# Second layers of a gated expert network on one core: two product sizes, one fp32 expert instead of three, and a reordered start of the first half

## The reference, cut to what matters

```python
B, L, DM, H, E, HD = (512, 64, 768, 4, 8, 384)
scores = einsum('bld,d->bl', x, aw); scores = where(x.sum(-1) != 0, scores, -inf)
feature = einsum('bl,bld->bd', softmax(scores), x)
g_h = relu(einsum('bd,hdk->bhk', feature, gW1) + gb1)
gate = softmax(einsum('bhk,hke->bhe', g_h, gW2) + gb2)[arange(b), D]
h1 = relu((einsum('bd,edk->ebk', feature, eW1) + eb1[:, None]) * inv1[:, None] + bn1_b[:, None])
h2 = relu((einsum('ebk,eko->ebo', h1, eW2) + eb2[:, None]) * inv2[:, None] + bn2_b[:, None])
rep = einsum('be,ebo->bo', gate, h2)
out = softmax((einsum('bo,hoc->bhc', rep, hW) + hb)[arange(b), D])
```

## Time and profile before

| what | value |
|---|---|
| median of 3 runs | 584.44 us (584.1 to 585.29) |
| the profiled execution's own time | 583.16 us |
| its span | 581.4 us |
| mean granted TensorE clock | 0.954 |
| PE busy | 515.3 us, 89% |
| DVE busy | 479.8 us, 83% |
| ACT busy | 460.1 us, 79% |
| POOL busy | 88.6 us, 15% |
| read from HBM | 167.32 MB |

### The profile page before, as it was taken

The page is one execution under the profiler, slowest core; times in us unless marked ns, Lnnn a source line. Parts: engine busy times, 40 slices in busy tenths (PEclk is TensorE's granted clock), DMA queues, the critical chain, the costliest instruction groups (busy, mean ns, idle before and its releaser), DMA issues.

```text
span 581.4 us, 10779 instructions
## 1 busy us (share of the span) xinstructions
PE 515.3 (89%) x3974; PEld 407.1 (70%) x3974; DVE 479.8 (83%) x917; ACT 460.1 (79%) x959; POOL 88.6 (15%) x130
## 2 busy tenths in 40 slices
PE   0476556879999999999999999999999999999995
PEld 0111112335987888878888888889889998999894
DVE  6899998998998897979999999664477686768673
ACT  5899999897999788988999899655566666666662
POOL 3100000002113020211121211112212222222200
PEclk9967888589999999999999999999999999999999
DMA  8999999998999999999999974545546756575620
GB/s 313 377 400 403 402 399 402 401 394 331 407 389 398 385 391 393 390 393 391 362 340 369 377 268 123 173 144 164 166 139 187 208 167 195 166 211 165 193 82 0
DMA packets 52053, 168.02 MB, mean 289 GB/s; under 512 B 4629, under 2 KB 4757, under 8 KB 52001
## 3 DMA queue, kind: packets, MB, share of 16 engines
q1 hardware_dynamic: 35344, 100.68, 45.2%
q0 software_dynamic: 16512, 66.27, 34.7%
q10 hardware_dynamic: 144, 0.39, 0.2%
HBM read 167.32 MB, written 0.00 MB: 288 GB/s over the span
## 4 chain that ended last, share of the span: by engine, by line
PE 49%; DMA 30%; DVE 14%; issue 5%; ACT 2%; SPq 0%; POOL 0%; DVEq 0%; ACTq 0%
DMA xring<-in_r_x_dram 29%; PE banks L957 9%; PE banks L947 8%; PE banks L949 8%; PE banks L948 8%; DVE prod_out L680 6%; PE banks L956 5%; DVE wlo L668 4%; PE banks L1034 4%; PE banks L1003 3%; PE banks L954 2%; PE banks L955 1%; DMA wraw<-in_L_rec_gW_dram 1%; DVE h L771 1%; ACT copy_out L457 1%
## 5 line engine op out<-in xcount | busy, mean ns | idle before, releaser
L680 DVE CUSTOM_DVE_ANT_0 prod_out<-xring,aw_bc 128x768 bf16<-128x768 f32 x256 | 233.3, 948 | 8.6 <-DMA xring<-in_r_x_dram 7.0
L457 ACT ACTIVATE copy_out<-xring 128x768 bf16<-128x768 f32 x256 | 212.8, 833 | 11.4 <-DMA xring<-in_r_x_dram 10.4
L668 DVE TENSOR_TENSOR wlo<-wraw,whi 128x1152 fp32r<-128x1152 f32 x106 | 142.6, 1351 | 32.9 <-ACT whi L442 32.8
L442 ACT ACTIVATE whi<-wraw 128x1152 fp32r<-128x1152 f32 x106 | 122.8, 1159 | 49.6 <-PE banks L949 27.2
L947 PE MATMUL banks<-feat,whi 128*128 128x256 f32 x432 | 124.6, 288 | 1.9 <-ACT h L499 0.6
L949 PE MATMUL banks<-feat,wlo 128*128 128x256 f32 x432 | 122.2, 283 | 0.0
L948 PE MATMUL banks<-feat,whi 128*128 128x256 f32 x432 | 122.1, 283 | 0.0
L1034 PE MATMUL banks<-xring,pwin 128*32 128x384 f32 (+1 forms) x1024 | 112.6, 579 | 9.6 <-ACT pwin L475 9.6
L422 POOL DMA_DIRECT2D wraw<-in_L_rec_eW_dram x90 | 68.5, 761 | 246.0 <-DVE wlo L668 240.1
L957 PE MATMUL banks<-feat,whi 128*128 128x512 f32 x240 | 86.4, 396 | 0.0
L947 PEld LDWEIGHTS banks<-feat,whi 128*128 128x128 f32 x432 | 82.8, 192 | 2.9 <-ACT w2raw L501 1.0
(11 more groups left out here) (118 smaller groups left out, 565.6 us busy)
## 6 DMA issues: line engine op xcount, KB each, us to landing
xring<-in_r_x_dram SPq DMA_DIRECT2D x128, 768.0 KB, 8.5
wraw<-in_L_rec_eW_dram POOLq DMA_DIRECT2D x90, 576.0 KB, 5.1
wraw<-in_L_rec_gW_dram POOLq DMA_DIRECT2D x16, 576.0 KB, 4.8
w2raw<-in_L_rec_eW_dram POOLq DMA_DIRECT2D x6, 576.0 KB, 8.4
aw_bc<-in_L_rec_aw_dram ACTq DMA_DIRECT2D x1, 384.0 KB, 5.4
w2raw<-in_L_rec_gW_dram POOLq DMA_DIRECT2D x1, 48.0 KB, 5.5
h<-in_L_rec_eb_dram POOLq DMA_DIRECT2D x1, 24.0 KB, 5.3
h<-in_L_rec_bn_g_dram POOLq DMA_DIRECT2D x1, 24.0 KB, 5.1
```

Source lines behind the costliest of these rows:

```text
L442: nc.scalar.activation(whi[:, split_slot(u), :, :], wraw[:, raw_slot(u), :, :], ACT.Copy).then_inc(hi_ready, 1)
L457: nc.scalar.activation(copy_out[:, t % 2, :], x_in[:, r % RING_ROUNDS, j, i, :], ACT.Copy, accum_out=rowsum[:, r % 2, t:t + 1]).then_inc(s ...
L668: nc.vector.tensor_tensor(wlo[:, split_slot(u), :, :], wraw[:, raw_slot(u), :, :], whi[:, split_slot(u), :, :].bitcast(F32), ALU.subtract) ...
L680: nc.vector.tensor_tensor_reduce(out=prod_out[:, t % 2, :], in0=x_in[:, r % RING_ROUNDS, j, i, :], in1=aw_bc[:, :], scale=1.0, scalar=0.0, ...
```

## The change

Four edits. `NATIVE` goes from 3 to 1, so experts 1 and 2 of chunk 0 get split second layers and the split experts' panel order. In chunk 1 the second-layer panels of experts 0 to 6 become wide; for that h1's high and low halves are put beside each other in one tensor (`h1s`), the tiles get a join on DVE, and the relu moves into the gating operation. Before the slot loop ACT and DVE get another order. The head's wait names another semaphore.

```diff
-NATIVE = 3
+NATIVE = 1
...
-            c, kind, _ = PANELS[panel]
-            return c == NCH - 1 and kind in "ab"
+            c, kind, q = PANELS[panel]
+            return c == NCH - 1 and kind in ("a" if q == E - 1 else "abc")
...
-        h1_hi = sb("h1_hi", [P, KT, CHUNK], F32R)
-        h1_lo = sb("h1_lo", [P, KT, CHUNK], F32R)
+        h1s = sb("h1s", [P, KT, 2, CHUNK], F32R)
+        h1_hi, h1_lo = h1s[:, :, 0, :], h1s[:, :, 1, :]
...
             softmax_exp(FIRST_ROUNDS - 1)
+            place_probs(FIRST_ROUNDS - 1)
             split_hi(0)
-            place_probs(FIRST_ROUNDS - 1)
             split_hi(1)
             copy_rows(1)
-            sum_rows(FIRST_ROUNDS, to_score(0)[:1])
             for g in range(2):
                 features_hi(1, g)
-            sum_rows(FIRST_ROUNDS, to_score(0)[1:])
+            sum_rows(FIRST_ROUNDS, to_score(0))
...
                 for m in range(MT):
-                    t = MT * "ab".index(kind) + m
+                    if kind == "c":
+                        part, col = h2[:, m, :], N1 + HT * q + m
+                    else:
+                        t = MT * "ab".index(kind) + m
+                        part, col = h1[:, t, :], KT * q + t
                     dve.wait_ge(part_ready, joined_count(panel, m))
-                    nc.vector.scalar_tensor_tensor(out=h1[:, t, :], in0=banks[:, bank_of(panel, m), 0:CHUNK],
-                                                   scalar=scale[:, KT * q + t:KT * q + t + 1], in1=h1[:, t, :],
+                    nc.vector.scalar_tensor_tensor(out=part, in0=banks[:, bank_of(panel, m), 0:CHUNK],
+                                                   scalar=scale[:, col:col + 1], in1=part,
                                                    op0=ALU.mult, op1=ALU.add).then_inc(joined, 1)
...
-                dve.wait_ge(z_read, read_count(panel_of(c, "c", q), MT - 1))
-                nc.vector.tensor_tensor(h2[:, :, :], h2[:, :, :],
-                                        gate_bc.unsqueeze(1).to_broadcast([P, HT, CHUNK]),
-                                        ALU.mult).then_inc(gated_ready, 1)
+                gates = gate_bc.unsqueeze(1).to_broadcast([P, HT, CHUNK])
+                panel = panel_of(c, "c", q)
+                if is_wide(panel):
+
+                    dve.wait_ge(joined, joined_count(panel, MT - 1))
+                    nc.vector.scalar_tensor_tensor(out=h2[:, :, :], in0=h2[:, :, :], scalar=0.0, in1=gates,
+                                                   op0=ALU.max, op1=ALU.mult).then_inc(gated_ready, 1)
+                else:
+                    dve.wait_ge(z_read, read_count(panel, MT - 1))
+                    nc.vector.tensor_tensor(h2[:, :, :], h2[:, :, :], gates, ALU.mult).then_inc(gated_ready, 1)
...
             split_lo(0)
-            split_lo(1)
             copy_rows(1)
-            score_tiles(FIRST_ROUNDS, to_score(0)[:1])
             for g in range(2):
                 features_lo(1, g)
-            score_tiles(FIRST_ROUNDS, to_score(0)[1:])
+            split_lo(1)
+            score_tiles(FIRST_ROUNDS, to_score(0))
...
-                        a_hi, a_lo = h1_hi, h1_lo
+                        a_hi, a_lo, a = h1_hi, h1_lo, h1s
                     else:
-                        a_hi, a_lo = feat_hi[:, c, :, :], feat_lo[:, c, :, :]
+                        a_hi, a_lo, a = feat_hi[:, c, :, :], feat_lo[:, c, :, :], feat[:, c, :, :, :]
...
-                            last = wide_products(bank, whi[:, slot, k, cols], wlo[:, slot, k, cols], feat[:, c, kk, :, :],
+                            last = wide_products(bank, whi[:, slot, k, cols], wlo[:, slot, k, cols], a[:, kk, :, :],
                                                  kk == 0, kk == KT - 1)
...
                 if c:
 
-                    pe.wait_ge(joined, joined_count(panel_of(c, "b", E - 1), MT - 1))
+                    pe.wait_ge(z_read, read_count(panel_of(c, "b", E - 1), MT - 1))
```

## The result

The changed kernel takes 587.5 us (median of 5 runs, 587.17 to 587.85) against 584.1 us (583.56 to 585.29): ratio 1.0058, 95% interval 1.0046 to 1.0069, so 3.4 us slower. The profiled execution took 587.46 us with a span of 585.6 us, 4.2 us longer than that of before.

What follows compares the result with a forecast made beforehand. The prediction took DVE's amount of work to set when slot 50 ends, with PE alone the bound later. Its terms, +5.5 - 1.2 + 0 = +4.3 us on 584.44, gave 588.7 us, range 583.6 to 593.

Steps and rivals of the forecast that it cites:

- What bounds the kernel: x's loads to 176 us, PE from 206 to 265, DVE's work from 265 to 362, PE alone from 450 to 560.
- the rival in which it can't: Before slot 50, DVE's idle time can't be used, so most of 16.3 us shows: +13.5, 598 us; chance 0.08.
- the one in which PE stays the bound: Between 206 and 362 us DVE's extra work is hidden and PE's savings count: -3.8 us, 580.6; chance 0.12.
- NATIVE and the layout: Before slot 50, 11.4 + 4.9 us more DVE work, less idle time and overlap, ends that slot 5.5 us later.
- the overlap: On DVE before slot 50, 20 added back-to-back instructions overlap by some 0.08 us each, taking off 1.6 us.
- The layout: DVE's copy to h1_hi slows from 548 to 958 ns; twelve copies before slot 50 add 4.9 us.
- The wide second layers: In chunk 1, wide second-layer panels save 1.0 to 1.5 us, taken as 1.2, with DVE's joins covered.
- The start: Reordering before the slot loop gives 0 (bounds -1.2 and +0.6), as a load of x ends the stretch at 175.6 us.
- Cost: nothing: In chunk 1, the wide second layers' joins and the relu inside the gating were claimed to cost nothing.
- Seven panels: Seven second-layer panels of chunk 1 were counted as becoming wide, saving 0.14 to 0.21 us each.
- The sum: Whole kernel: +5.5 before slot 50, -1.2 in chunk 1 and 0 for the start make +4.3 us.
- The level: Whole kernel: the profiled 583.16 lies 1.3 us below the median, so +4.3 was added to 584.44, giving 588.7 us.

Runs made afterwards that it cites:

- e10: The changed kernel with NATIVE = 4, one-run h1 halves in chunk 0 and the old order before the slot loop: 581.62 us, ratio 0.9962 to the kernel before.
- e11: The kernel before with NATIVE = 1 and nothing else: 584.58 us against 583.91 beside it, ratio 1.0014.
- e1: The changed kernel with h1's halves as single runs again in chunk 0: 582.78 us, ratio 0.9983 to the kernel before.
- e7: The kernel before with the new order before the slot loop and nothing else: 584.55 us, ratio 1.0000.
- e8: The kernel before with the last expert's second first-layer panel narrow and nothing else: 582.86 us, ratio 0.9969.
- e5: The changed kernel with h1 padded by 8 elements behind each run of 256: 583.81 us, ratio 0.9988 to the kernel before.
- e6: The kernel before with h1's halves side by side (h1s) and nothing else: 587.01 us, ratio 1.0045.
- e2: The changed kernel with NATIVE back to 3: 584.14 us, ratio 1.0004 to the kernel before.

## Why the prediction was right, and where it was off

*What bounds the kernel.* Right in the direction that mattered. DVE's amount of work set the time to slot 50, its idle time between 206 and 265 us took the first 9 us of new work, and PE's 2.6 us of savings were swallowed. PE's loss from 16 to 51 plus those 2.6 makes 7.9 us of new gaps; "about 8" was forecast. (The idle time that the profile shows for PE there grew from 1.4 to 7.9, by 6.5; the ends of matmuls are modelled, so the starts are the better count.) DVE's idle time could be used almost to the end, 8.8 of 9.9 us, which rules out the rival in which it can't, and PE's gaps rule out the one in which PE stays the bound. My sentence that "a microsecond taken from PE between 265 and 362 us is therefore worth nothing, and one given to DVE costs one" stands. Its mirror, which I had for e10, that relief of DVE is worth as much, doesn't.

*NATIVE and the layout.* Forecast together +5.5, measured +5.25. By parts: 0.9 without the slow copies, measured 0.92 and 0.93 in e11 and e1; twelve slow copies 4.9 on DVE, measured 4.3 on the path. One count in it is wrong: the added instructions on DVE are 12 and not 20 (four `wlo`, four copies, four subtractions; e11 has 929 instructions on DVE where 917 were). By the same 0.08 us each the overlap is 1.0 and not 1.6, and the term would have been +6.1. So +5.5 is near the measured value partly because of a slip.

*The layout.* The price of the copy was not in the trace of before. I took 958 ns, measured were 937. By the rule of the Trainium skill's page "VectorE: DVE Perf Modes", section "What auto-detection actually checks", 768 against 3 keeps an operation at one element a cycle, and 3 against 3 doesn't; this case's traces agree, with 937 and 674 ns. The Trainium skill's page "Vector Engine (DVE) Microarchitecture Reference", section "5.1 Performance modes — why throughput varies by op and dtype", adds that the first port takes the larger half of an odd outermost count. That would account for 674 rather than 548; this case has the one number for it.

*The wide second layers.* -1.2 forecast, -0.95 measured. The mechanism was right, joins covered as read from the earlier trace rows, PE without a wait behind them. The size was a little off: the first of the seven panels saved 0.19 us and each of the others 0.13, at or just under the low end of my range, while the first-layer panels beside them, already wide, kept their sum to 0.01 us.

*The start.* Forecast 0 by the loads' end at 175.6 us, and e7 measured 0, within 0.8 us either way. That it is the loads that take the early start back is argued from the waits in e7's trace and not shown by an experiment.

*What was missed.* "Cost: nothing" and "Seven panels" overlook that `is_wide` in the new kernel says `"a" if q == E - 1`: the last expert's `b` panel becomes narrow. I read the line for what it adds and not for what it takes away. It costs PE 0.2 us and takes three joins, ACT's copy and two hand-overs out of the chain before the last unit: -1.36 us in the traces, -1.4 in e8. It is also what the other wait of the head belongs to. This step of the sum is simply absent, and with it the forecast would have been +2.9. It also puts DVE's fifteenth copy right before the last unit, where I had written that the copies behind slot 50 have room.

*The sum.* +5.25 - 0.95 - 1.36 = +2.9 us, and the start within its spread; measured are +3.4 with an interval of 2.7 to 4.0. The forecast of +4.3 lies above that interval, by the term that it lacks: with it, it would have been 0.5 too low, without it it was 0.9 too high. That it still came near is partly luck: the missing term would have taken 1.4 off, and a right count of the overlaps would have added 0.6.

*The level.* I added the change to the median of before, 584.44, because the profiled execution, 583.16, lay 1.3 us under it. In that trace unit 9 came earlier than in all six others with the old order, which had it 0.15 to 1.50 us later. So its low time was most likely the luck of one execution, and the span of the changed kernel, itself at its median, differs from it by 4.2 us where the medians differ by 3.4. The forecast of 588.7 is 1.2 above the measured 587.5: 0.9 by the change and 0.3 by the median, which was 584.44 in the runs shown and 584.1 in those beside the changed kernel.

## What to carry to other kernels

A layout is part of an instruction's price: before two tiles are put side by side for the engine that profits, look for an instruction in the trace that runs faster than its neighbours of the same size, and ask whether its source and destination keep their form. Where two engines are both nearly full, work added to the fuller one costs nearly its full length at once, and work taken back pays only down to the second engine's limit. When a condition in a diff is rewritten, list what it stops to select as well; here the one panel that left the list gained more than the seven that joined it.

## What the runs showed of the hardware that I hadn't expected

A DVE copy of 768 fp32 elements between SBUF tiles took 543 to 552 ns (medians of e1, the kernel before and e8) with one run on both sides, 674 ns (e5) with three runs of 256 with gaps on both sides, and 935 to 943 ns (the changed kernel, e6, e2) with one run in the source and three in the destination. Of these three forms the slow one is that in which the two sides differ; gaps alone didn't make it slow.

PE's pace on a second-layer unit was not the same in all traces: with h1 padded in e5, a narrow unit took about 0.15 us less than in every other trace. PE doesn't read h1 there but `h1s`, whose shape was the same, and the cause is open.
